# A decoder kernel on one core: a norm's two variances in one VectorE operation, the slot's base folded into its sum, the token number counted up on Pool

## What is computed

```python
x = _layernorm(x + _L0_attn_ref(x, qkv_w, qkv_b, out_w, out_b))
x = _layernorm(x + _L0_xattn_ref(x, ctx_1024, ctx_1024, W_proj, b_proj))
x = _layernorm(x + _L0_ffn_ref(x, wg, W1, b1, W2, b2))

def _layernorm(x, axis=-1, eps=1e-05):
    m = jnp.mean(x, axis=axis, keepdims=True)
    v = jnp.var(x, axis=axis, keepdims=True)
    return (x - m) / jnp.sqrt(v + eps)

# in _L0_ffn_ref
    top1 = jnp.argmax(scores, axis=-1)
    rank = jnp.take_along_axis(jnp.cumsum(oh, axis=0), top1[:, None], axis=1)[:, 0] - 1
    valid = rank < capacity
    slot = jnp.where(valid, top1 * capacity + rank, trash)
    buf = jnp.zeros((E * capacity + 1, D), dtype=x.dtype).at[slot].set(xf)
```

## Time and profile before

| | |
|---|---|
| median of 3 runs | 418.44 us (415.81, 418.44, 419.33) |
| profiled execution | 417.75 us |
| its span, first to last instruction | 416.0 us |
| mean granted TensorE clock | 0.983 of full speed |
| batch loop | about 8 to 325 us |
| experts | about 325 to 403 us |

### The profile page before, as it was taken

The page is one execution under the profiler, slowest core; times in us unless marked ns, Lnnn a source line. Parts: engine busy times, 40 slices in busy tenths (PEclk is TensorE's granted clock), DMA queues, the critical chain, the costliest instruction groups (busy, mean ns, idle before and its releaser), DMA issues.

```text
span 416.0 us, 19194 instructions
## 1 busy us (share of the span) xinstructions
PE 389.4 (94%) x7065; PEld 294.6 (71%) x7065; DVE 328.2 (79%) x1645; ACT 268.7 (65%) x609; POOL 252.6 (61%) x372
## 2 busy tenths in 40 slices
PE   7989999999999999999999999998878999999970
PEld 6647777777777777777777767766566788888860
DVE  6366688988889888888988988977875478877880
ACT  4536777777877677787778777776756544445560
POOL 5344455676676676666677667476564037777683
PEclk9999999999999999999999999999998999999995
DMA  3900000111201010111111114000011566666100
GB/s 110 321 26 17 23 23 16 29 28 30 57 27 30 28 29 28 43 42 29 28 31 28 38 35 135 9 24 14 17 50 49 141 126 149 153 146 165 52 30 15
DMA packets 44674, 24.69 MB, mean 59 GB/s; under 512 B 19417, under 2 KB 40719, under 8 KB 44582
## 3 DMA queue, kind: packets, MB, share of 16 engines
q1 hardware_dynamic: 42246, 19.27, 17.7%
q0 software_dynamic: 2336, 4.20, 3.1%
HBM read 14.43 MB, written 9.58 MB: 58 GB/s over the span
## 4 chain that ended last, share of the span: by engine, by line
PE 82%; issue 5%; POOL 4%; DVE 2%; DMA 2%; ACT 2%; SPq 1%; POOLq 1%; DVEq 0%; ACTq 0%
PE banks L789 13%; PE banks L739 13%; PE banks L1214 9%; PE banks L1200 8%; PE banks L731 8%; PE banks L751 7%; PE banks L724 6%; PE banks L801 3%; PE banks L868 2%; PE banks L817 2%; PE banks L769 2%; PE banks L770 2%; PE banks L771 2%; PE banks L912 1%; POOL expert_in L520 1%
## 5 line engine op out<-in xcount | busy, mean ns | idle before, releaser
L1730 DVE TENSOR_REDUCE mx<-banks 128x8 f32<-128x1024 f32 x64 | 77.0, 1219 | 19.5 <-PE banks L739 19.5
L1278 ACT ACTIVATE arena<-banks 128x1024 f32<-128x1024 f32 x64 | 62.1, 1021 | 41.1 <-PE banks L739 41.1
L789 PEld LDWEIGHTS banks<-arena,V 128*32 128x32 f32 x2048 | 53.1, 109 | 29.8 <-ACT arena L1308 23.6
L789 PE MATMUL banks<-arena,V 128*32 128x128 f32 x2048 | 67.0, 275 | 0.6 <-ACT arena L1308 0.3
L1308 ACT ACTIVATE arena<-banks 128x1024 f32<-128x1024 f32 x64 | 62.1, 1022 | 6.0 <-PE banks L731 6.0
L1531 ACT ACTIVATE arena<-banks,b1T 128x321 f32<-128x321 f32 x64 | 33.8, 528 | 39.4 <-PE banks L1200 38.7
L487 POOL TENSOR_TENSOR rs<-ve,minus_half 128x1 f32<-128x1 f32 x32 | 18.1, 567 | 54.7 <-DVE ve L1698 54.7
L656 POOL DMA_INDIRECT out_x<-ot,idx x40 | 40.3, 1007 | 18.1 <-issue 9.0
L504 POOL TENSOR_TENSOR rs<-ve,minus_half 128x2 f32<-128x2 f32 x32 | 23.2, 725 | 38.6 <-DVE ve L1718 38.5
L520 POOL DMA_INDIRECT expert_in<-x,sidx x32 | 35.2, 1099 | 16.6 <-DVE x L1804 5.6
L1214 PEld LDWEIGHTS banks<-w_sb,arena 128*128 128x128 f32 x320 | 37.7, 192 | 3.1 <-issue 1.8
(11 more groups left out here) (216 smaller groups left out, 968.7 us busy)
## 6 DMA issues: line engine op xcount, KB each, us to landing
w_sb<-in_L_ffn_W SPq DMA_DIRECT2D x16, 256.0 KB, 3.2
EB<-expert_in SPq DMA_DIRECT2D x9, 325.0 KB, 4.8
expert_in<-zeros SPq DMA_DIRECT2D x10, 266.5 KB, 3.3
X<-in_x SPq DMA_DIRECT2D x32, 64.0 KB, 1.9
C<-in_ctx SPq DMA_DIRECT2D x32, 64.0 KB, 2.8
out_x<-fb SPq DMA_DIRECT2D x32, 64.0 KB, 2.1
EQ<-expert_in SPq DMA_DIRECT2D x24, 80.0 KB
out_x<-ot,idx POOLq DMA_INDIRECT x40, 2.2
```

The source lines that it names most:

```text
L789: mm = pe.matmul(bank(name)[VW * s:VW * (s + 1), half * P:(half + 1) * P], V[:, h, :], scored[:, h // NA, h % NA, :], start=q == 0, stop=q ...
L1278: nc.scalar.activation(A1[b % 2][:, 2 * half:2 * half + 2].rearrange("p j a t -> p j (a t)"), pair("s1", half), ACT.Relu).then_inc(s1_out[ ...
L1730: v.tensor_reduce(mx[b % 2][:, 8 * half:8 * half + 8].rearrange("p (j a) -> p j a", a=NA), pair("s2", half).rearrange("p j (a t) -> p j a ...
```

## The change

- The two variances are one `scalar_tensor_tensor`: (constant columns) x variance + (constant columns). The constants, 1 and eps, and 1 + eps and eps squared, are set once by four memsets.
- slot0 is gone. slot1 is now rank - 656 x top, and the constant 8 x 656 - 1 is added as a second step in the operations that read it (address, minus_slot, one-hot).
- The token number is counted up on Pool in `op_x2`, ahead of the normalization and behind its waits, instead of in `op_rk4` on VectorE.

```diff
+        ve_scale = sb("ve_scale", [P, 2])
+        ve_shift = sb("ve_shift", [P, 2])
-        slot0 = sb("slot0", [P, 1])
...
                 wait(pool, scattered[b % 4], 16 * (b // 4))
+                if b >= 4:
+                    token = x2[b % 4][:, TOKEN:TOKEN + 1]
+                    g.tensor_scalar(token, token, float(4 * P), None, ALU.add)
                 g.tensor_scalar(x2[b % 4][:, 0:D], r2[:], mv2[:, 0:1], rs2[:, 0:1], ALU.subtract, ALU.mult).then_inc(x2_ready, 1)
...
             v.memset(eps[:], LN_EPS)
+            for k, (scale, shift) in enumerate([(1.0, LN_EPS), (1.0 + LN_EPS, LN_EPS * LN_EPS)]):
+                v.memset(ve_scale[:, k:k + 1], scale)
+                v.memset(ve_shift[:, k:k + 1], shift)
...
-                v.tensor_scalar(ve2[:, 0:1], mv2[:, 1:2], LN_EPS, None, ALU.add)
-                v.tensor_scalar(ve2[:, 1:2], mv2[:, 1:2], 1.0 + LN_EPS, LN_EPS * LN_EPS, ALU.mult, ALU.add).then_inc(
-                    var2_ready, 1)
+                v.scalar_tensor_tensor(out=ve2[:], in0=ve_scale[:], scalar=mv2[:, 1:2], in1=ve_shift[:], op0=ALU.mult,
+                                       op1=ALU.add).then_inc(var2_ready, 1)
...
-                v.tensor_scalar(slot0[:], top[k][:], -float(CAPP), float(E * CAPP - 1), ALU.mult, ALU.add)
...
-                v.tensor_scalar(slot1[:], slot0[:], rank[b % 2][:], None, ALU.add).then_inc(slot1_ready, 1)
+                v.scalar_tensor_tensor(out=slot1[:], in0=top[b % 2][:], scalar=-float(CAPP), in1=rank[b % 2][:], op0=ALU.mult,
+                                       op1=ALU.add).then_inc(slot1_ready, 1)
...
-                v.tensor_scalar(sidx[b % 4][:], slot1[:], over[:], None, ALU.add)
+                v.tensor_scalar(sidx[b % 4][:], slot1[:], over[:], SLOT0, ALU.add, ALU.add)
                 if LATE <= b < B - 1:
-                    v.tensor_scalar(minus_slot[:, b - LATE:b - LATE + 1], slot1[:], 1.0 if b == LATE else -1.0, None, ALU.mult)
-                if b >= 4:
-                    token = x2[b % 4][:, TOKEN:TOKEN + 1]
-                    v.tensor_scalar(token, token, float(4 * P), None, ALU.add)
+                    sign = 1.0 if b == LATE else -1.0
+                    v.tensor_scalar(minus_slot[:, b - LATE:b - LATE + 1], slot1[:], sign, sign * SLOT0, ALU.mult, ALU.add)
...
-                v.tensor_scalar(hot[B - 1 - LATE][:, r0:r1], slot_of[:, r0:r1], slot1[:], None, ALU.is_equal).then_inc(hot_last, 1)
+                v.tensor_scalar(hot[B - 1 - LATE][:, r0:r1], slot_of[:, r0:r1], slot1[:], SLOT0, ALU.subtract,
+                                ALU.is_equal).then_inc(hot_last, 1)
```

More of the change, by code:

```diff
@@ L71, in decoder @@
     LATE = B - 4
+    SLOT0 = float(E * CAPP - 1)
     LATE_BANKS = (2, 3)
```

## The result

The changed kernel takes 421.75 us, the median of 11 executions (418.66 to 422.9), beside 418.24 us for the kernel before in 11 executions on the same chip: a ratio of 1.0085, 95% interval 1.0056 to 1.0113. That is 3.5 us, too little to be called slower by 1%, but clearly not zero, and outside the range that was forecast (416.2 to 421.0). A second measurement of the unaltered file, taken apart, gave 1.0106 (1.0064 to 1.0147). The profiled execution took 421.46 us with a span of 419.7, before 417.75 and 416.0: 3.7 us to explain.

A forecast was written before the change was run, and what follows sets the result against it. TensorE was taken to bound the kernel, with real idle time only in the last batches. The loop's -0.64 and the last batches' +0.25 gave -0.4 us, forecasting 418.0 us from the median 418.44, range 416.2 to 421.0.

The forecast's parts named there:

- The bound: Whole kernel: TensorE, busy 94% of the span, bounds it; only the last batches, 237 to 325.3 us, hold real idle time.
- The pause and the variance: Loop: VectorE pauses 0.33 us each 128th instruction, between the variances every second batch, losing 1.24 us; merging cuts this to 0.60.
- Rival B: Loop: the wandering pause hits the sensitive stretch more often than counted; +1.1 us, 419.5 us; chance 0.14.
- -0.64 + 0.25: Whole kernel: the loop's gain plus the last batches' net cost, summed to -0.4 us.
- The token: Pool, between root and x2: the token addition takes 0.15 us, near the iota; bounds 0.08 and 0.53 us.
- rival A: Pool ahead of x2: the token operation is long; t = 0.4 gives +3.4 us, upper bound 0.53 gives +5.9; chance 0.16.
- My own formula for A: Batches 4 to 19 and three direct places: 16(t - 0.22) + 3t - 0.2 + 0.74 - 1.24, t the token's added time.
- The loop: Batches from 109 to 237 us: loses 0.60 us to pauses instead of 1.24, so -0.64 us.
- The slot's edits at nothing: VectorE's address and one-hot operations: the added second arithmetic step costs nothing, bounds 0 and 0.05 us.
- The last batches: Batches 22, 26 and 31 meet x2 directly: three times 0.15, +0.45, less 0.2 from shorter VectorE sequences, net +0.25 us.
- the 0.02 for what I don't see: Whole kernel: the chance of 0.02 left for causes outside the forecast and its rivals.

The follow-up runs named there:

- variance_only: The kernel before with the two variances in one operation and nothing else; 418.93 us.
- token_back: The changed kernel with the token number counted up on VectorE again; its loop from batch 4 to batch 19 takes 133.81 us.
- after_sp14: The changed kernel with fourteen satisfied waits on SyncE ahead of the early rows' transfer; 1.0075 of the kernel before.
- token_only: The kernel before with the token number counted up on Pool ahead of x2 and nothing else; 419.11 us.
- token_early: The changed kernel with the token operation on Pool moved ahead of the wait for the variance; median 418.8 us.

## Why the prediction was wrong

*The bound.* Right. The loop has no idle time to speak of, TensorE's busy time in each stage is the same to 0.6 us, and the only stage that grew is the one with real idle time.

*The pause and the variance.* Right in mechanism, a third too large. One operation of 0.217 us, no "issue" gap before it; 1.24 us were to be won before the pauses that move elsewhere, and variance_only and token_back show 0.7 to 0.9. Rival B, pauses that cost more as they wander, falls with the same two runs. What failed is that the gain was carried to the end: "-0.64 + 0.25" adds it to the last batches as if nothing lay between, and by batch 23 it is gone in both runs.

*The token.* The term was mis-sized: 0.15 us forecast, 0.237 added. I took the iota, the nearest row below, and every arithmetic row of Pool with few columns was above 0.25, as rival A said. My own formula for A gives, at t = 0.237, 16 x 0.017 + 3 x 0.237 - 0.2 + 0.74 - 1.24 = +0.3 us. Its part for the loop, 0.27 + 0.74 - 1.24 = -0.23, fits the measured -0.17. Its part for the last batches, 3t less 0.2, is +0.51, and what is measured there up to batch 30, +1.04, is another thing: token_back, without the operation on Pool, has +0.91 there. So rival A's mechanism holds in the loop, and by itself it would have left the time inside the range.

*The loop.* Forecast -0.64, measured -0.17 (134.40 against 134.57): gain and price nearly cancel.

*The slot's edits at nothing.* The term "I take nothing, bounds 0 and 0.05 us" failed. I looked at the length of the new form, which is right (0.150 us), and not at what runs beside it on Pool: at batch 22 it lasts until Pool's QE ends, 1.48 us, and TensorE idles 1.23 us. In the loop with the token on Pool the edits are worth 0.7 to 1.1 us the other way (hidden in what the other parts cost).

*The last batches.* Here the prediction failed most. "Three times 0.15 is +0.45", less 0.2, is +0.25 us. From batch 19 to batch 30 it is +1.04, most of it the step at batch 22; batch 31 adds 2.6 us. I had named batch 31 as one that meets x2 directly, but asked only what Pool does ahead of x2 and not what Pool itself waits for there: a transfer of 325 KB, on the critical path with 2.6 us, in the same DMA engines as the instruction fetch. The earlier trace rows show batch 31 without the wait behind it. Neither forecast nor rival had it, and the 0.02 for what I don't see was far too little in a stage with 7.8 us of idle time.

*The Trainium skill.* "Runtime: NRT & Kernel Launch", section "Instruction fetch mechanics", says that a sequencer fetches its next page of 16 KB by a DMA queue of its own while it executes the current one. The trace agrees for TensorE: 57 packets of 16 KB on a queue of their own. What I had not drawn from it is that a queue of its own is not a DMA engine of its own: the tail above is a sixteenth of the rows.

*Settled and open.* Shown: where the 3.7 us of the profiled execution are; that the slot's sum holds TensorE up at batch 22 in every kernel that has it; that moving TensorE's block boundaries gives 2.45 us back; that the rows are late in all profiles in which the fetch lies in them and in no other. Open: how much of the 2.45 us is the fetch's and how much the clock's; why the whole change has 23 of its 25 executions (three measurements, after_sp14 among them) above 419.5 us, and token_only, variance_only, token_back and token_early two to six of 12. An execution above 419.5 us without a trace isn't proof of the fetch either.

## What to carry to other kernels

An operation moved to another engine has to be placed as well as counted: 0.24 us of Pool ahead of x2 cost most of what the loop had gained (0.6 of 0.8 us), the same operation ahead of a wait cost 0.2 us (133.99 us for the loop, with the token on VectorE 133.81). An operation in a new form has to be looked at beside what the other engines do in the same moment, row by row: the mean of 0.192 us hid one row of 1.48 that idled TensorE. Where a transfer is on the critical path, look in the view of transfers for what else its DMA engines carry in these microseconds, instruction packets too, and look for a tail at a few GB/s. And when a kernel's time moves by more than any of its edits can explain, move the block boundaries of its instructions with a few satisfied waits in the setup and measure again before anything is said of the edits; and compare the granted clock of the executions, as the waits move that too.

## What the hardware showed that I had not expected

An instruction fetch of 16 KB takes 0.9 to 1.5 us in most cases, and 1.7 to 2.3 in seven of the eight profiles in which it lies in the rows (in the eighth 0.97, and the rows still land 3.7 us after their issue); the packets of its DMA engine wait behind it, one sixteenth of the transfer, and the transfer counts as landed only with them. A single 128x1 addition of a constant takes 0.245 us on Pool; VectorE's operations of that size are at 0.14 to 0.2. One `scalar_tensor_tensor` of 128x1 on VectorE, 0.150 us by itself, takes 1.48 to 1.63 us beside Pool's QE and ends with it.
